# Taking the statistics of a later group's layer norm during an earlier group, in a four-group transformer kernel on one core

## What is computed

```
x = x + L0_xattn(_layernorm(x), ctx, ctx, mask)     # 16 heads, ALiBi, softmax
x = x + L0_ffn(_layernorm(x))                        # shared expert and routed experts
x = x + L1_xattn(_layernorm(x), ctx, ctx)            # 16 heads by 16 heads, inside a row
x = x + L1_ffn(_layernorm(x))                        # 8 experts, two per row
... (layers 2 and 3)

def _layernorm(x, eps=1e-5): (x - mean(x)) / sqrt(var(x) + eps)   # over the 256 columns of a row
```

## Time and profile before

| | us |
|---|---|
| median of 3 runs | 1708.67 (1707.65 to 1715.27) |
| the profiled execution, its own time | 1716.88 |
| its span, first to last instruction | 1715.1 |
| PE busy | 1327.7 (77%) |
| DVE busy | 832.6 (49%) |
| ACT busy | 433.3 (25%) |
| POOL busy | 287.6 (17%) |

### The profile page before, as it was taken

The page is one execution under the profiler, slowest core; times in us unless marked ns, Lnnn a source line. Parts: engine busy times, 40 slices in busy tenths (PEclk is TensorE's granted clock), DMA queues, the critical chain, the costliest instruction groups (busy, mean ns, idle before and its releaser), DMA issues. The chain is left out here.

```text
span 1715.1 us, 26091 instructions
## 1 busy us (share of the span) xinstructions
PE 1327.7 (77%) x8177; PEld 1078.8 (63%) x8189; DVE 832.6 (49%) x2298; ACT 433.3 (25%) x1098; POOL 287.6 (17%) x306
## 2 busy tenths in 40 slices
PE   5877587685636248998988786877439999999997
PEld 3554444453423147888875565655329999999996
DVE  2258868778778731221233848485632222222222
ACT  2635245244112001111132232322101111111111
POOL 2010030020100020000023435351421111111111
PEclk9786686588777579999988898888759999999999
DMA  9992010010192258888820011100047888888884
GB/s 343 346 289 61 1 62 0 0 61 0 39 310 95 98 203 290 289 296 297 293 67 25 17 33 38 37 26 13 25 180 278 318 315 314 313 317 313 313 315 165
DMA packets 116307, 291.38 MB, mean 170 GB/s; under 512 B 8192, under 2 KB 90528, under 8 KB 101024
## 3 DMA queue, kind: packets, MB, share of 16 engines
q1 hardware_dynamic: 106032, 273.00, 45.5%
q0 software_dynamic: 10224, 17.77, 4.1%
HBM read 218.84 MB, written 71.90 MB: 170 GB/s over the span
## 5 line engine op out<-in xcount | busy, mean ns | idle before, releaser
L725 PE MATMUL bank<-norm_cols,work 128*128 128x128 f32 x3744 | 461.8, 277 | 20.8 <-DMA work<-in_moe 19.6
L725 PEld LDWEIGHTS bank<-norm_cols,work 128*128 128x128 f32 x3744 | 449.0, 193 | 38.8 <-issue 21.5
L1536 DVE TENSOR_TENSOR extra<-bank,span 128x256 f32<-128x256 f32 x234 | 99.2, 425 | 465.1 <-ACT span L1343 465.1
L725 PE MATMUL bank<-work,extra 128*128 128x256 f32 x936 | 240.0, 380 | 0.0
L1343 ACT ACTIVATE span<-bank 128x256 f32<-128x256 f32 x234 | 89.9, 384 | 541.9 <-PE bank L725 523.4
L725 PEld LDWEIGHTS bank<-work,extra 128*128 128x128 f32 x936 | 160.4, 191 | 12.5
L2634 POOL DMA_INDIRECT out_x<-att_rows,slot_token x39 | 60.7, 1556 | 378.0 <-ACT att_rows L1353 313.6
L2455 POOL TENSOR_TENSOR rstd<-var_eps,neg_half 128x4 f32<-128x4 f32 x17 | 17.3, 1018 | 501.6 <-DVE var_eps L1548 501.6
L725 PE MATMUL bank<-weights,norm_cols 128*128 128x512 f32 (+1 forms) x192 | 89.2, 614 | 12.2 <-ACT norm_cols L1374 5.5
L725 PE MATMUL bank<-work 128*128 128x256 f32 (+4 forms) x260 | 70.7, 418 | 28.0 <-ACT work L1374 12.7
L1280 ACT ACTIVATE work<-bank,row_max 128x128 f32<-128x128 f32 x256 | 69.8, 392 | 41.2 <-DVE row_max L1598 41.1
(11 more groups left out here) (330 smaller groups left out, 1965.6 us busy)
## 6 DMA issues: line engine op xcount, KB each, us to landing
work<-in_moe SPq DMA_DIRECT2D x78, 1024.0 KB, 7.5
work<-in_moe SPq DMA_DIRECT2D x39, 2048.0 KB, 7.8
work<-in_moe SPq DMA_DIRECT2D x39, 512.0 KB, 6.1
expert_rows_in<-zero SPq DMA_DIRECT2D x3, 5590.0 KB, 47.1
expert_rows_in<-zero SPq DMA_DIRECT2D x3, 5504.0 KB, 36.0
expert_rows_out<-zero SPq DMA_DIRECT2D x3, 5504.0 KB, 33.7
att_cols<-expert_rows_in SPq DMA_DIRECT2D x39, 130.0 KB, 2.0
att_cols<-expert_rows_in SPq DMA_DIRECT2D x39, 128.0 KB, 3.3
```

Source lines behind the costliest of these rows:

```text
L725: return pe.matmul(o, l, r, start=a, stop=z)
L1536: return dve.tensor_tensor(o, a, b, op)
```

## The change

The twelve tiles of groups 1 to 3 get their mean and variance during group 0. There the list of pieces, empty before, now holds twelve statistics, three aggregations of four tiles, and one addition of the epsilon; the first statistics piece waits for the three loads of x. POOL makes one power of all twelve columns. In groups 1 to 3 the first norm copies its four columns of mean, variance and power out of the twelve and applies them. The counts of the semaphores follow.

```diff
-STEPS = {"phase1": 142,  "moe3": 14, "last": 16}
+STEPS = {"phase1": 136,  "moe3": 14, "last": 16}
...
-        neg_half = sb("neg_half", [P, T])
+        neg_half = sb("neg_half", [P, FIRST])
...
+        STX = sb("stats_later_groups", [P, FIRST, 6])
+        MVX = sb("mean_var_later_groups", [P, FIRST, 2])
+        VEX = sb("var_eps_later_groups", [P, FIRST])
+        RSX = sb("rstd_later_groups", [P, FIRST])
+        MVG = sb("mean_var_of_group", [P, T, 2])
+        RSG = sb("rstd_of_group", [P, T])
...
+            def later_stats():
+
+                def stats(t):
+                    if t == 0:
+                        dve.wait_ge(sem("x_loaded"), 16 * (GROUPS - 1))
+                    d(dve.bn_stats(STX[:, t, :], X[:, (T + t) * D:(T + t + 1) * D]))
+
+                def means(part):
+                    settle()
+                    alone()
+                    for t in part:
+                        d(dve.bn_aggr(MVX[:, t, :], STX[:, t, :]))
+
+                def variances():
+                    settle()
+                    dve.tensor_scalar(VEX[:, :], MVX[:, :, 1], 1e-5, None, ALU.add).then_inc(sem("variance_later"), 1)
+
+                pieces = [lambda t=t: stats(t) for t in range(FIRST)]
+                pieces += [lambda n=n: means(range(T * n, T * (n + 1))) for n in range(GROUPS - 1)]
+                return pieces + [variances, "end"]
+
+            def first_norm(g):
+
+                dve.wait_ge(sem("rstd_later"), 1)
+                d(dve.tensor_copy(MVG[:, :, :], MVX[:, ds((g - 1) * T, T), :]))
+                d(dve.tensor_copy(RSG[:, :], RSX[:, ds((g - 1) * T, T)]))
+                settle()
+                for t in range(T):
+                    i = dve.tensor_scalar(XN[:, t, :], xg(g, t), MVG[:, t, 0:1], RSG[:, t:t + 1], ALU.subtract, ALU.mult)
+                    if t < T - 1:
+                        d(i)
+                i.then_inc(sem("normed"), 1)
+
             def phase1(plan, turn, g, prev):
-                norm(lambda t: xg(g, t), lambda t: XN[:, t, :], 1e-5, 2 * g + 1, "normed")
-                left = Pieces([] if prev is None else layer1_pieces(prev, 2 * prev + 1, prev + 1) + layer1_rows_out(prev, 2 * prev + 2))
+                if prev is None:
+                    norm(lambda t: xg(g, t), lambda t: XN[:, t, :], 1e-5, 1, "normed")
+                else:
+                    first_norm(g)
+                left = Pieces(later_stats() if prev is None else layer1_pieces(prev, 2 * prev + 1, prev + 1) + layer1_rows_out(prev, 2 * prev + 2))
...
             def phase1(plan, turn, g, prev, sent=None):
-                power(2 * g + 1)
-                if prev is not None:
+                if prev is None:
+                    power(1)
+                else:
                     power(2 * prev + 1, "_l1")
                     if sent is not None:
                         scatter(sent, NA)
                 x_bias(g)
                 if prev is not None:
                     power(2 * prev + 2, "_l1")
-                power(2 * g + 2)
+                else:
+                    pool.wait_ge(sem("variance_later"), 1)
+                    pool.tensor_tensor(RSX[:, :], VEX[:, :], neg_half[:, :], ALU.pow).then_inc(sem("rstd_later"), 1)
+                power(g + 2)
```

More of the change, by code:

```diff
@@ L1630, in phase1 @@
                 alone()
-                norm(lambda t: xg(g, t), lambda t: XN[:, t, :], 1e-5, 2 * g + 2, "normed")
+                norm(lambda t: xg(g, t), lambda t: XN[:, t, :], 1e-5, g + 2, "normed")
                 if prev is not None:
@@ L2454, in power @@
                 pool.wait_ge(sem("variance" + stream), count)
-                pool.tensor_tensor(RS[:, :], VE[:, :], neg_half[:, :], ALU.pow).then_inc(sem("rstd" + stream), 1)
+                pool.tensor_tensor(RS[:, :], VE[:, :], neg_half[:, 0:T], ALU.pow).then_inc(sem("rstd" + stream), 1)
             def powers(count):
@@ L2481, in query_power @@
                 pool.wait_ge(sem("variance_q"), g + 1)
-                pool.tensor_tensor(RSQ[:, :], VEQ[:, :], neg_half[:, :], ALU.pow).then_inc(sem("rstd_q"), 1)
+                pool.tensor_tensor(RSQ[:, :], VEQ[:, :], neg_half[:, 0:T], ALU.pow).then_inc(sem("rstd_q"), 1)
             def scatter(turn, rows, rows_to=xs_dram):
```

## The result

The change made the kernel slower. Its median is 1718.36 us (15 runs, 1712.17 to 1725.56) against 1708.67 us of the kernel before (15 runs, 1701.56 to 1719.45); the ratio is 1.0047, 95% interval 1.0027 to 1.0068, that is 8.0 us on 1708.67. The forecast of 1708.7 us, range 1703.5 to 1715.5, with a chance of 0.05 for slower, is wrong.

A forecast was written before the change was run, and what follows sets the result against it. DVE's long stretch was taken to bound groups 1 to 3, starting when PE's first scores allow. Groups 1 to 3, group 0 and POOL each summed to 0, so 1708.7 us against the median, range 1703.5 to 1715.5.

The forecast's parts named there:

- The step on groups 1 to 3: First norms of groups 1 to 3: apply starts 2.9 us earlier each, 8.8 us in all, costed at nothing.
- the removed 2.9 us a group: First norm of groups 1 to 3: 3.35 us to the apply's start falls to about 0.42 us of copies and settle.
- the 8.4: Forecast DVE idle time in us ahead of group 2's first score maximum, after the change.
- the 5.50 us: DVE's idle time ahead of group 2's first score maximum in the kernel before, read as a wait for PE.
- Group 0, added on DVE: Twelve statistics, three aggregations, one addition in group 0, about 6 us with settles; taken as 0, bounds 0 and +1.4 us.
- PE's way to its first scores: Group 0: DVE's ten statistics end at 36.9 us, 2.7 us ahead of the first maximum at 39.61 us.
- The step on POOL's queue: Groups 1 to 3 on POOL: layer 1's power, scatters and bias addition all move 2.9 us earlier; no gain or loss.
- The load wait: Rival in group 0: a late x load holds DVE's first maximum, slipping all by 9.9 us to 1718.6; chance 0.05.
- the bound of 33.4: Group 0: latest time in us by which the three x loads were to land, ahead of DVE's statistics.
- The slip of unit 1: Rival in group 0: second maximum and exponentials stay behind by 1.4 us, not hidden, giving 1710.1; chance 0.07.
- the one that was given 0.05: Slower rival in group 0: DVE's new wait for the x load delays the first maximum, 1718.6 us; chance 0.05.

The follow-up runs named there:

- kernel 2: The changed kernel with 64 DVE instructions that only add to a semaphore put in group 0 behind the first norm; 1703.13 us median, ratio 0.9972.
- kernels 4 and 9: The changed kernel with 64 DVE semaphore increments in group 0 and POOL's bias addition ahead of its scatters, in two batches; ratios 0.9959 and 0.9994.
- both controls: The kernel before, unchanged, measured twice more; ratios 1.0007 and 1.0001.
- the kernels with 14 and with 92: The kernel before with 14 or 92 DVE semaphore increments added in group 0; stretch 315.75 us with 14, ratio 1.0019 with 92.
- Kernel 3: The changed kernel with POOL's bias addition moved ahead of the eight scatters; 1706.04 us median, ratio 0.9986.
- the three kernels with the loop at 137: Loop starting at DVE instruction 137: the changed kernel, it with the bias addition ahead of the scatters, the kernel before with 28 increments; ratios 1.0047, 0.9986, 1.0036.
- the loop at 187 and 189: Loop start by DVE instruction: the changed kernel with 50 increments (187), the kernel before with 80 (189); 1726.43 and 1721.87 us, one run each.
- kernel 1: The kernel before with 28 DVE semaphore increments added in group 0 behind the first norm; 1713.7 us median, ratio 1.0036.

## Why the prediction was wrong

**The step on groups 1 to 3.** "It is costed at nothing for the end time" was right in its own terms: with the loop at a good place the removed 2.9 us a group go into the waits, 3.0, 6.8 and 6.6 us in kernel 2, and the stretch stays at 315.1 us. In kernels 4 and 9 (315.1 and 315.2 us) the waits of groups 2 and 3 are 4.5 to 4.9 us, because the addition there lies beside the query norm. Group 2's wait in kernel 2 is 1.6 us short of the 8.4 because the 5.50 us that it was reckoned from were those of one execution: in four more profiles without a stall (both controls, the kernels with 14 and with 92) it was 4.14 to 4.31 us.

**The step that failed** is *Group 0, added on DVE*, and its last sentence, "Cost nothing; the cover is PE's way to its first scores". It priced the 28 instructions by the time that they run and held that against the cover. They had a second price, that of their place in DVE's instruction stream: 6.25 and 5.90 us at the loop's two back edges, where the kernel before has 0.59 and 0.56. No duration row shows that; the number of the loop's first instruction and the packets of q14 do.

**The step on POOL's queue** failed with it. It put the bias addition of group 2 at 246.6 us, "inside DVE's idle time"; it came at 252.89. The prediction named the mechanism itself, a DVE operation that takes 2 us more beside the addition, and set its price to nothing because all moved earlier. Kernel 3 shows that this collision, with what follows on PE, is how the stall gets to the end time: without it the stretch is 315.70 us, so 9.9 of the 10.1 us are gone.

**The rivals.** The load wait never showed: the x load released DVE at 31.75, ahead of the bound of 33.4. The slip of unit 1 took place, the second maximum 3.34 us behind the first for 1.60 (3.0 was forecast), and was hidden as far as can be told: the third exponentials start 8.01 us behind the first maximum and 6.86 before, but that varies from 6.7 to 7.7 us without the change and from 6.8 to 8.0 with it, and the way from group 0's first maximum to group 1's is 90.3 to 93.6 us in the eight profiles without the change and 90.5 to 93.5 in the six with it. The slower case that came was not among them; the one that was given 0.05 has another place and price.

**The sign of the profiled pair** is another lesson: 1716.88 and 1713.18 us say "faster", the ratio of all runs "slower by 0.47%".

## What to carry to other kernels

Code added ahead of a loop can cost more than its time: it moves the loop. Where a loop of DVE is some 300 instructions long, as here, compare the first instruction behind its back edge before and after. A wait of 5 to 6 us "<-issue" just there, together with packets on the instruction queue in the later turns, means that instructions are fetched again; a few dozen empty increments in idle time tell whether it is the place. Then ask what a late engine pushes in the others' queues: a stall within its cover cost 10 us here because a POOL addition came to lie beside DVE's products, and changing the order of two POOL steps took that away. And take a wait that an estimate rests on from more than one execution: group 2's was 5.50 us in one and 4.2 in the others.

## What the runs showed of the hardware that was not expected

- The wait at a back edge: 5.3 to 6.3 us in the six places of the three kernels with the loop at 137 (5.0 to 6.2 at 187 and 189), with five packets of the instruction queue in the turn behind it (six once), and none in the kernels without the wait; with the loop at 187 and 189, 1.5 to 2.0 us more a few instructions on.
- POOL's addition of 128x1024 (2.35 us) made a DVE product of 128x768 take 3.67 us for 0.96, one of 128x256 2.50 for 0.41, and in kernel 1 one of 128x1024 2.47 for 1.22; the maximum beside it in the kernel before (251.10, the addition from 249.53 to 251.89) keeps its 1.29.
- The power of 12 columns on POOL took 2.29 us, that of 4 columns 1.02; by these two, an estimate of 0.16 us a column and 0.4 fixed.
